# One kernel, three edits: q computed feature-major instead of being turned, the turn of the targets between the halves of an up product, and one output bias behind the state copy

## What is computed

```python
q = silu(x @ Wq)                      # 512x512
k = x @ Wk;  k = k * rsqrt(sum(k*k) + eps)
v = x @ Wv;  beta = 2 * sigmoid(x @ Wbeta);  gate = x @ Wg1 @ Wg2
for each chunk of 16 tokens, in order:        # S carries over
    kh = k_i @ S;  target = v_i - k_i
    v_new = backward of layernorm(kh) against target
    A = tril(q_i @ k_i.T) * beta_i
    qh = q_i @ S - A @ v_new
    o_i = q_i + layernorm(qh)
    S = S - (k_i * beta_i).T @ v_new
x = x + layernorm(rmsnorm(o * sigmoid(gate)) * norm_w @ Wo)
h = silu((x' @ Wgate) * gs) * ((x' @ Wup) * us)      # 512 -> 1536, x' = layernorm(x)
out = x + layernorm((h @ Wdown) * ds)
```

## Time and profile before

| | |
|---|---|
| median of 3 runs | 886.61 us (886.08 to 890.05) |
| the profiled execution | 886.27 us, of which 884.5 us is the span |
| PE busy | 794.7 us, 90% of the span |
| DVE, ACT, POOL busy | 77%, 56%, 54% |
| mean granted TensorE clock | 0.963 of full speed |

### The profile page before, as it was taken

How to read it: one execution, slowest core, us unless ns; L and a number is a source line. 1 busy time by engine, 2 the same in 40 slices (tenths; PEclk the granted TensorE clock), 3 DMA queues, 4 the chain that set the end, 5 groups by cost and what they waited for, 6 DMA issues and landing times.

```text
span 884.5 us, 23061 instructions
## 1 busy us (share of the span) xinstructions
PE 794.7 (90%) x8364; PEld 560.3 (63%) x8364; DVE 677.3 (77%) x2704; ACT 496.8 (56%) x1328; POOL 481.2 (54%) x848
## 2 busy tenths in 40 slices
PE   8877777698989999999999999999999999978896
PEld 4453444456567666667676676766676767766795
DVE  3778887887877887778787878778777878767444
ACT  2776675767557665655656475656565564623331
POOL 5455756575555656556565546565655646445300
PEclk9998899898989999999999999999999999979998
DMA  8012121211211001000100010000100010001000
GB/s 274 25 50 60 38 60 37 61 37 37 61 37 37 2 2 49 2 25 3 49 2 26 1 38 14 26 1 2 50 2 26 2 49 2 2 1 48 1 25 24
DMA packets 16721, 28.48 MB, mean 32 GB/s; under 512 B 3520, under 2 KB 3520, under 8 KB 16608
## 3 DMA queue, kind: packets, MB, share of 16 engines
q1 hardware_dynamic: 16608, 27.02, 10.0%
HBM read 22.82 MB, written 4.19 MB: 31 GB/s over the span
## 4 chain that ended last, share of the span: by engine, by line
PE 58%; DVE 16%; POOL 10%; ACT 8%; issue 6%; SPq 1%; DMA 1%; POOLq 0%; DVEq 0%; ACTq 0%
PE bank L632 18%; PE bank L426 15%; PE bank L665 8%; PE bank L583 3%; POOL rho L1188 3%; PE bank L440 3%; PE bank L608 3%; PE bank L560 2%; ACT BDk L901 2%; PE bank L569 2%; PE bank L591 2%; DVE work L1500 2%; DVE f L1582 1%; PE bank L454 1%; DVE work L1504 1%
## 5 line engine op out<-in xcount | busy, mean ns | idle before, releaser
L1188 POOL TENSOR_TENSOR rho<-sy,cst 128x2 f32<-128x2 f32 x128 | 89.7, 701 | 233.8 <-DVE sy L1473 233.8
L583 PEld LDWEIGHTS bank<-VX,BDkR 128*64 128x64 f32 x1024 | 44.6, 138 | 84.7 <-issue 39.2
L1516 DVE TENSOR_TENSOR SQ<-SQ,bank 128x128 f32<-128x128 f32 x128 | 36.7, 286 | 76.8 <-PE bank L583 75.8
L583 PE MATMUL bank<-VX,BDkR 128*64 128x64 f32 x1024 | 56.3, 231 | 35.4 <-DVE VX L1509 35.2
L956 ACT ACTIVATE qhR<-bank 128x64 f32<-128x64 f32 x128 | 28.2, 221 | 100.7 <-PE bank L591 100.1
L915 ACT ACTIVATE BDkR<-kR,cst 128x128 f32<-128x128 f32 x256 | 81.4, 397 | 0.0
L665 PE MATMUL bank<-DW,fh 128*128 128x512 f32 x188 | 80.4, 427 | 0.6 <-DVE fl L1589 0.6
L901 ACT ACTIVATE BDk<-bank 32x256 f32<-32x256 f32 x124 | 46.5, 375 | 54.7 <-DVE kR L1415 46.1
L665 PE MATMUL bank<-DW,fl 128*128 128x512 f32 x188 | 75.3, 400 | 0.0
L1495 DVE SCALAR_TENSOR_TENSOR work<-work,rho,rR 128x32 f32<-128x32 f32 x256 | 53.1, 248 | 26.4 <-POOL rho L1188 26.3
L569 PE MATMUL bank<-SQ,BDq 128*64 128x32 f32 x1024 | 54.0, 226 | 17.7 <-ACT qhR L956 16.5
(11 more groups left out here) (170 smaller groups left out, 2159.8 us busy)
## 6 DMA issues: line engine op xcount, KB each, us to landing
xt<-in_x SPq DMA_DIRECT2D x16, 256.0 KB, 2.8
x<-in_x SPq DMA_DIRECT2D x16, 256.0 KB, 2.8
out<-x SPq DMA_DIRECT2D x16, 256.0 KB, 2.1
yb<-in_gate_w SPq DMA_DIRECT2D x12, 256.0 KB, 2.8
yb<-in_up_w SPq DMA_DIRECT2D x12, 256.0 KB, 2.7
yb<-in_down_w SPq DMA_DIRECT2D x12, 256.0 KB, 2.7
Wk<-in_wk SPq DMA_DIRECT2D x1, 1024.0 KB, 6.6
Wv<-in_wv SPq DMA_DIRECT2D x1, 1024.0 KB, 8.7
```

What stands on the lines that cost most here:

```text
L583: ins = mm(dS[p, e], bdkr[:, gh, j % 4, p], VX[:, e], start=True, stop=True, skip_group_check=True)
L1188: tt(dst, src, cst[:, C_NH:C_NH + n], ALU.pow).then_inc(*one)
L1516: tt(S, S, dS.rearrange("p (g e) -> p g e", e=DH), ALU.add).then_inc(*scan_v.one("S"))
```

## The change

**Edit 1, q by feature.** `queries` computes q turned: 128x64 pieces of Wq are the weights and 128 tokens of `xnT` the stream, 32 matmuls where `proj` had 8. ACT's silu then writes a feature-major `qfeat`, `prep_qT` on TensorE goes, and ACT's copies to `qT` and DVE's transpose to `qR` read `qfeat` in SBUF instead of a bank.

**Edit 2.** From the preparation of tile 4 on, the targets' turn `prep_dT` stands between the two halves of the up product, not ahead of both.

**Edit 3.** In odd tiles the bias of the second output tile, `fin_yc(..., 1)`, moves on ACT from ahead of the last `take_qh` to chunk 0 of the next tile, behind its copy of q into `SQ`.

```diff
-        qtok = kn = thT = sb("q_kn_th", D)
+        qfeat = kn = thT = sb("q_kn_th", D)
...
+            def queries(b, blocks):
+                for m in blocks:
+                    for k in range(KD):
+                        for lo in HALVES:
+                            e = k * D + m * P
+                            ins = mm(b[lo, m * P:(m + 1) * P], Wq[:, e + lo.start:e + lo.stop],
+                                     xnT[:, k * P:(k + 1) * P], start=(k == 0), stop=(k == KD - 1),
+                                     skip_group_check=True)
...
             def prep_q(t, blocks=range(4)):
...
-                ins = proj(PA[0][:, :], Wq, D, blocks)
+                queries(PA[0], blocks)
...
-            def prep_qT(t):
-                pe.wait_ge(*prep_a.at("q", t))
-                if begun(t - 3):
-                    pe.wait_ge(tail_v.sem, tail_v.at("x1", t - 3))
-                turn(PA[1], qtok, prep_t.one("qT"))
...
             def prep_vv(t, last):
...
-                    pe.wait_ge(*prep_v.at("qR", t))
+                    if begun(t - 3):
+                        pe.wait_ge(tail_v.sem, tail_v.at("x1", t - 3))
...
                     if j == 6:
+                        if 2 in ffn:
+                            ffn_u(*ffn[2], 0)
                         if prep and not early(t + 1):
                             prep_dT(t + 1)
                         if 2 in ffn:
-                            ffn_u(*ffn[2], 0)
                             ffn_u(*ffn[2], 1)
...
-                    if j == 2 and prep:
-                        prep_qT(t + 1)
...
-                proj(G[:, :], Wq, D, (0, 1))
+                queries(G, (0, 1))
...
-                pe.wait_ge(*prep_a.at("q", 0))
-                turn(G, qtok, prep_t.one("qT"))
...
-            def prep_qT(t, s, b=PA[1]):
-                act.wait_ge(*prep_t.at("qT", t))
+            def prep_qT(t, s):
+                act.wait_ge(*prep_a.at("q", t))
...
                     if j == 0 and t == 0:
                         x_norm(1)
+                        act.wait_ge(*prep_v.at("qR", 0))
...
                     if j == 0:
+                        if not s and is_pair(h - 3):
+                            fin_yc(2 * (h - 3) + 1, 1)
...
                         if fin:
                             fin_yc(2 * (h - 2), 0)
-                            fin_yc(2 * (h - 2) + 1, 1)
...
-            def prep_qR(t, s, b=PA[1]):
-                dve.wait_ge(*prep_a.at("qT", t))
+            def prep_qR(t, s):
+                dve.wait_ge(*prep_a.at("q", t))
```

More of the change, by code:

```diff
@@ L199, in build @@
         prep_a = Each(sem, "prep_a", "xnT q ksq qT g1 beta BDk rT th")
-        prep_t = Each(sem, "prep_t", "xnT q k qT v kT2 kT1 g1 beta dT gate cen brow")
+        prep_t = Each(sem, "prep_t", "xnT q k v kT2 kT1 g1 beta dT gate cen brow")
         root_g = Steps(sem("root_g"), "kse rk")
@@ L468, in prep_xnT, with prep_q @@
                 turn(PA[0], xn, prep_t.one("xnT"))
-            def prep_q(t, blocks=range(KD)):
+            def queries(b, blocks):
[6 more added lines that the diff above has]
+                                     skip_group_check=True)
+                if 3 in blocks:
+                    ins.then_inc(*prep_t.one("q"))
+            def prep_q(t, blocks=range(4)):
                 if 0 in blocks:
                     pe.wait_ge(*prep_a.at("xnT", t))
-                ins = proj(PA[0][:, :], Wq, D, blocks)
-                if KD - 1 in blocks:
-                    ins.then_inc(*prep_t.one("q"))
+                queries(PA[0], blocks)
             def prep_beta(t):
@@ L485, in prep_k @@
                     if 0 in blocks:
-                        pe.wait_ge(*(prep_a.at("rT", t - 1) if t > 1 else prep_v.at("qR", 0)))
+                        pe.wait_ge(*(prep_a.at("rT", t - 1) if t > 1 else prep_a.at("q", 0)))
                     ins = proj(G[:, :], Wk, D, blocks)
@@ L827, in prologue @@
                 turn(U4, dv, prep_t.one("dT"))
-                proj(G[:, :], Wq, D, (2, 3)).then_inc(*prep_t.one("q"))
+                queries(G, (2, 3))
                 pe.wait_ge(*prep_v.at("bx", 0))
@@ L859, in prep_q @@
                     act.wait_ge(*prep_v.at("thR", t - 1))
-                fn(qtok[:, :], PA[0][:, :], ACT.Silu).then_inc(*prep_a.one("q"))
+                fn(qfeat[:, :], PA[0][:, :], ACT.Silu).then_inc(*prep_a.one("q"))
             def take_g1(b):
@@ L885, in prep_qT @@
                         ins = fn(qT[s][64 * a:64 * a + 64, 256 * gp:256 * gp + 256],
-                                 b[64 * gp:64 * gp + 64, 256 * a:256 * a + 256], ACT.Copy)
+                                 qfeat[64 * gp:64 * gp + 64, 256 * a:256 * a + 256], ACT.Copy)
                 ins.then_inc(*prep_a.one("qT"))
@@ L1031, in drain @@
                 if t == NT:
+                    fin_yc(2 * (p - 2) + 1, 1)
                     post_qsq(n, n % 2)
@@ L1170, in prologue @@
                 act.wait_ge(*prep_t.at("q", 0))
-                fn(qtok[:, :], G[:, :], ACT.Silu).then_inc(*prep_a.one("q"))
-                prep_qT(0, 0, G)
+                fn(qfeat[:, :], G[:, :], ACT.Silu).then_inc(*prep_a.one("q"))
+                prep_qT(0, 0)
                 chunk_q(0, 0, 0)
@@ L1415, in turn @@
                 nc.vector.transpose(rows(dst), feat(src)).then_inc(*one)
-            def prep_qR(t, s, b=PA[1]):
-                dve.wait_ge(*prep_a.at("qT", t))
+            def prep_qR(t, s):
+                dve.wait_ge(*prep_a.at("q", t))
                 if begun(t - 2):
                     dve.wait_ge(post_v.sem, post_v.at("o", t - 2))
-                turn(qR[s], b, prep_v.one("qR"))
+                turn(qR[s], qfeat, prep_v.one("qR"))
             def prep_kn(t):
                 dve.wait_ge(root_g.sem, root_g.at("rk", t))
-                dve.wait_ge(*prep_t.at("qT", t))
+                dve.wait_ge(*prep_a.at("qT", t))
                 tt(heads(kn), heads(G if early(t) else PA[0]), wide(rk[:, :]), ALU.mult).then_inc(*prep_v.one("kn"))
@@ L1706, in body @@
                     if j == 0 and t == 0:
-                        prep_qR(0, 0, G)
+                        prep_qR(0, 0)
                     if j == 1 and scan:
```

## The result

The changed kernel took a median of 876.12 us (874.69 to 876.97, 4 runs) against 888.09 us (886.08 to 890.05, 4 runs) for the kernel before: a ratio of 0.9859, with a 95% interval of 0.9836 to 0.9883. Its profiled execution took 875.81 us, of which 874.0 us is the span; before, these were 886.27 and 884.5. So 10.46 us went in the two executions that the traces show, where the prediction had 9.6. The medians lie 11.97 us apart, but the four executions of the kernel before differ by 4.0 us among themselves, so what follows goes by the traces.

The account below looks back on a forecast made before the run. The prediction took PE to bound tiles 5 to 14. Its terms, -1.1 (prologue), -4.4 and -0.4 (targets' turn), -4.0 (bias), -1.0 (turn of q) and +1.3 (query product), gave -9.6 us, so 877 us, range 871 to 883.

Parts of the forecast that it names:

- What bounds the kernel: In tiles 5 to 14 a microsecond on PE is one of the kernel, if what it meets next is ready.
- Edit 2, 0.44 us per tile: Tiles 5 to 14: PE's hole before the targets' turn is filled until ACT's `rT` is late; 4.4 us in all.
- The 0.4 us allowed for tiles 3 and 4: The same hole before the targets' turn in tiles 3 and 4, allowed a gain of 0.2 us each.
- Edit 3, 0.8 us per pair: Ends of tiles 5, 7, 9, 11, 13: L569 waits less for the copy of qh; 4.0 us in all.
- ACT itself comes about 0.22 us earlier through edit 2: Odd tiles' ends: `th` waits for a gate product that ends sooner, so qh is out at about 521.05.
- The turn of q: Removing it gains 0.2 us in tiles 6, 8, 10, 12 and 14, nothing in odd ones; 1.0 us in all.
- The query product: 32 matmuls in place of 8 cost 0.12 us per tile in eleven preparing tiles from 4 on; +1.3 us.
- Rival B: In the query product 24 more weight loads are exposed, 1.45 us per tile in eleven tiles: 891.4 us; chance 0.04.
- Rival A: PE's holes only move, as later write steps wait for `VX`: 883.8 us; chance 0.14.
- The prologue, -1.1: Without the turn of q, ACT's copies to `qT` start at once behind silu, gaining 1.1 us before the first read.
- The sum: All terms over the whole kernel: -9.6 us from the profiled 886.27, so 876.7, stated as 877 for the median.
- Rival C: Rounding tiles gain too, as filled holes keep PE's clock up; half of some 10 us back gives 871.7; chance 0.12.

Follow-up runs that it names:

- e1: The kernel before with only the targets' turn moved between the halves of the up product: 883.07 us, ratio 0.9937.
- e2: The kernel before with only the second output bias moved behind the state's copies in the next tile: 882.74 us, ratio 0.9933.
- e3: The kernel before with only q computed by feature and its turn removed: 885.1 us, ratio 0.9966.
- e5: The changed kernel with the targets' turn behind both halves of the up product: 877.77 us, ratio 0.9866.
- e4: The changed kernel with an unread turn of q put back at its old place in tiles 4 to 14: 876.79 us, ratio 0.9879.
- e6: The changed kernel with idle matmuls, one pair ahead of the first read and three ahead of the first write: 875.67 us, ratio 0.9847.
- e7: The changed kernel with idle matmuls in tiles 0 to 3, 45 pairs ahead of writes and 11 between reads: 871.52 us, ratio 0.9807.
- e9: The changed kernel run once more, without alteration, for a second profile: 877.59 us in one execution.

## Why the prediction was right, and where its terms were off

**What bounds the kernel:** right. From tile 5 to tile 14 a hole that is filled on PE is kept up to the next late chain, and e1, e2 and e3 add up there.

**Edit 2, 0.44 us per tile:** right in size and cause. e1 has 0.39 to 0.45, and L460 waits for `rT` as foreseen. e5 shows that the turn has nearly half an up product of slack and no more. The 0.4 us allowed for tiles 3 and 4 is borne out as well as one profile can: e1 has -0.37 at chunk 7 of tile 3, and -0.63 and then +0.53 in tile 4.

**Edit 3, 0.8 us per pair:** the mechanism was right, the size 0.2 short. The step that failed was "ACT itself comes about 0.22 us earlier through edit 2", by which qh would be out at 521.05, too late for an L560 that has moved 0.44. But in the changed kernel ACT moved as far as PE: the first bias stands 520.33 - 515.65 = 4.68 us ahead of its place in the earlier trace rows, and the read 521.17 - 516.49 = 4.68 ahead of its own in the earlier trace rows. `take_qh` also starts 0.09 us before the bias ends. So it is out as the read begins, with edit 2 as without it, and edit 3 gives all that there is: L569 stood 1.23 us behind L560 and can follow by 0.24, a difference of 0.99, of which the runs show 1.00. Nor is the 0.22 there with edit 2 alone: in e1 the five waits shrink by 0.4 us together, 0.08 each. Five times 1.00 is 5.0, and not 4.0.

**The turn of q, 0.2 in even tiles and nothing in odd ones:** right; 0.25 and 0.00. e4 puts the turn back and loses it the same way, with the odd tiles' gain eaten by `xl`.

**The query product, +0.12:** right in sign, half in size: +0.06, for 32 matmuls in 3.62 us, 0.113 each. Rival B is refuted: 24 more weight loads in a row stay hidden. The changed kernel's groups by line and form count them, two for each matmul of the program:

```profile
L476 PE MATMUL bank<-xnT,Wq 128*64 128x128 f32 x1024 | 64.8, 287 | 1.4 <-ACT xnT L851 1.4
L476 PEld LDWEIGHTS bank<-xnT,Wq 128*64 128x64 f32 x1024 | 60.6, 146 | 2.7 <-ACT xnT L851 2.0 <-issue 0.7
```

A load lasts 146 ns, and in the 3.62 us of a product 64 of them start, one every 57 ns, so they run under the matmuls. The rival's price was read too low, by the way: the 256 loads of the earlier trace rows belong to 128 matmuls, so 24 more matmuls bring 48 loads of 60 ns, 2.9 us per tile and not 1.45. That the product grew by 0.06 refutes it all the more. The rule of the Trainium skill that the prediction weighed (TensorE: Matmul & The Clock Gate, Part 3, "What overlaps and what doesn't"), that loads overlap only for other rows of the array, doesn't hold for these loads.

**Rival A,** that the holes only move, is refuted by the view of PE's waits: no write waits for `VX` in tiles 5 to 14.

**The prologue, -1.1, and tiles 3 and 4, -0.4:** the weak terms. Counted from Wk's product, the prologue gave 0.85. The other profiles agree: from that product to the first read are 17.82 to 18.27 us in the three with the old prologue (before, e1, e2) and 17.01 to 17.42 in the seven with the new one (all others but e6). The copies to `qT` do start at once, 0.03 us behind silu, but last 0.15 longer; most of what is missing of the 1.1 is that. The read itself didn't come earlier, because Wk's product began 0.84 us later in this execution. In e3 the first read came 0.69 us earlier. The larger miss was to add these microseconds to the sum at all. From the first read on the executions differ by more than the forecast, with the clock: by the read of chunk 2 of tile 0 1.6 us were lost at half clock, and by tile 4 they were back. The prediction's "in earlier tiles PE has room" is true of its waits, but not of its clock.

**The sum:** for the -9.98 us of the steady tiles -8.2 were forecast, for the -0.20 of the early ones -1.4, and for tile 15 and the drain, which gave -0.28, nothing. The total of 876.1 against 877 is therefore closer than its parts: an error of 1.8 us one way met one of 1.2 the other way. The base was luck too: 877 counts from a median of 886.61, and with a fourth execution that median is 888.09, 1.5 us higher.

**Rival C** described a cost that exists. The change didn't take it away (0.90 over the first 280 us, where it was 0.91), but e7 did: 871.5 us against the 871.7 that the rival named. The agreement is chance in part, since that figure assumed half of 10 us and e7 recovered some 4.6.

What stays open is the variation of the early stretch. The time at which Wk's product begins, 8.4 to 10.5 us in these profiles, and the times at which the clock falls differ from one execution to the next for the same code, and no run separates the two. The step of -0.23 at chunk 4 of tile 15, most of what tile 15 and the drain gave, isn't steady either: e9, the same code, has +0.03 there.

## What to carry to other kernels

Where one engine is unbroken, price a removed wait by the next chain that is late, and read that from the starts of the instructions on both sides: a waiting instruction's distance from the one before it, now and without the wait, is the gain, whatever other edits shift. Subtract the starts of a recurring instruction in two traces; where the steps repeat, edits can be told apart and added up, and where they don't, look at the granted clock before looking at the code. Here holes of about a microsecond on TensorE, in a stretch where it is idle a fifth of the time, were worth filling with idle matmuls into a free bank: all 56 pairs gave some 4 us, the first four at most 1.

## What was not expected of the hardware

**The clock in short holes.** After waits of 0.85, 1.05 and 1.30 us PE ran at 1.2 GHz (granted 0.50) from 30 to 36 us, and the same 24 matmuls took 4.44 us there and 2.67 with the holes filled. Fifty-six pairs of idle matmuls in tiles 0 to 3 brought the mean clock from between 0.958 and 0.964 (four executions) to between 0.981 and 0.986 (five), and the median time from 876.1 to 871.5 us. Four pairs out of these brought 1 us at most, within what executions differ by; the later falls of the clock stayed.

**The source of ACT's copies.** The four copies of a 64x256 tile to `qT` take 1.70 us from SBUF, where the earlier trace rows had 1.55 from a bank. Over all 64 copies the mean is 413 ns against 377: the "some tens of ns" of the prediction, but four in a row on the path of the prologue. ACT of the changed kernel, silu and the copies:

```profile
23.90 0.60 ACT L1177 ACTIVATE q_kn_th<-bank 128x512 f32<-128x512 f32 x1 [0.74 <-PE bank L476]
24.53 1.70 ACT L888 ACTIVATE qT<-q_kn_th 64x256 f32<-64x256 f32 x4
```
